# Row-sum reciprocals of an attention kernel sent through device memory instead of turned on TensorE, and the end of its perceptron done by row tile

## The chip, the cores and the metric

One Trainium2 chip, one core of it. The time is the device time of one execution in microseconds (us); a kernel is judged by the median of its runs. The engines are TensorE (PE: matrix products and turns, that is transposes, into PSUM), VectorE (DVE), ScalarE (ACT), GpSimd (POOL) and SyncE (SP), which issues all the transfers of this kernel, in program order, on one queue.

## What is computed

A decoder layer on x of 16 x 256 x 512 (self-attention, cross-attention on ctx_2048, each with 16 heads of 32 channels, then a perceptron of 512 to 2048 to 512), and behind it a "non-local" layer that multiplies by matrices made of ctx_2048. All in float32. Cut to what matters:

```
scores = einsum('bhqd,bhkd->bhqk', q, k) / sqrt(32)
scores = scores * mask - 10000.0 * (1.0 - mask)
probs  = softmax(scores)              # exp(s - max) / sum over the keys
ctx    = einsum('bhqk,bhkd->bhqd', probs, v)
x = x + merge_heads(ctx) @ w_o + b_o          # once for self-, once for cross-attention
x = x + gelu(layernorm(x) @ w1 + b1) @ w2 + b2
theta = theta_w @ x + theta_b ; out = gain * (w_w @ g^T phi^T theta / 512) + shift + x
```

The division by the sum is done last: the kernel weighs v with the raw exponentials, and multiplies the 32 channels of each head by 1/sum of their row. The sums stand with rows on the partitions, the weighed values with channels on the partitions, so the reciprocals must change sides.

## The kernel before

**Precision.** Every product of matrices is three products: each operand is split in a high part (`_h`) and the rest (`_l`), and `product` (L66 to L68) issues high*high, low*high and high*low.

**Blocks and slots.** The work is cut into 16 blocks k of two batches (512 rows): blocks 0 to 7 are self-attention, 8 to 15 cross-attention; k = 16 ends the last one. Each block has 8 slots h. In a slot every engine does, for several overlapping groups (a group is 4 heads of one batch, 128 groups in all), its next step: TensorE turns the exponentials of one group (L867, `turn`), does two units `a_` and `b_` of the projections (L66 to L68), scores a later group (L850), and weighs v with the turned exponentials (L880, `weigh`). Blocks 10 to 14 are one loop on the chip, the others are written out. The order within a slot is written by hand in the function `slot` of each engine, and waits are semaphores.

**PSUM.** Two banks, `banks`, go round: `a_`, `b_`, `own` (weigh), and so on. With three units in a slot, the bank that `weigh` filled in one slot is the one that `b_` needs in the next. `b_` therefore waits for `cx_ok`, which VectorE gives once it has read the weighed values out (`scaled`, L1384).

**Reciprocals.** In slot n VectorE takes the reciprocals of the 8 sums of each row (`inverses`, L1378, 128x8). GpSimd repeats each 32 times (`widen`, L657, tile `rwide`). At the end of `weigh` TensorE turns the two 128x128 halves of `rwide` into the free half of the bank (L884). In slot n+1 ScalarE copies them to `rt` (`sums_out`, L1112), and VectorE multiplies (`scaled`), ScalarE and VectorE split the result (`weighed`, L1118 and L1391).

**VectorE in a slot**: `mask_scores` part 0 (L1361), `inverses`, `scaled`, `maxima` part 0 (L1371), `weighed`, `mask_scores` part 1, the units' outputs, `maxima` part 1. TensorE's scores wait until both parts of `mask_scores` have emptied the PSUM tile `sc`.

**SyncE.** In slot 0 of a block it loads the rows of the block after it (`load_rows`, L441, four of 256 KB), in the cross-attention blocks also the context (`load_context`, L447, two of 512 KB) and the mask (`load_mask`, L452). `load_res` (L456) brings the rows that a result is added to, `store` (L460) writes the result.

**End.** After the attention come 8 bodies of the perceptron. After the last product of the last body VectorE adds four row tiles (L1587), ScalarE and VectorE split two batches of them and the two last `m1` matrices (`split_t`, L1246 to L1550), TensorE does `theta` and `last_product`, VectorE `last_out` (L1564), which for the last batch waits until the tile `res` has been stored.

Of the kernel before, what the change touches and what calls it, by code (L numbers as in the profile page):

```python
# [11 lines left out]
P = 128  # L12
# [125 lines left out]
def whole_network(nc, ctx, nl, m1t_dram, rows, x1, x2, ctx_t, s_mask, x_mask, s_weights, x_weights, fold_wt, columns, ln_biases,  # L138
# [19 lines left out]
    with ExitStack() as stack:  # L158
# [17 lines left out]
        b2_row = room.sb("b2_row", [P, 3 * H])  # L176
# [31 lines left out]
        with ExitStack() as shared:  # L208
            rt = shared.enter_context(nc.sbuf_tensor("A_rt", [P, S], F32))
        rwide = room.sb("rwide", [P, TPB, HPG, HD])  # L210
# [20 lines left out]
        w_s = rwide[:, :, :, :].rearrange("p t j d -> p t (j d)")  # L231
# [52 lines left out]
        def operands(b, end=False):  # L284

            whole = t_sb[:, b * TPB:(b + 1) * TPB, :]
            if end and b == BPB - 1:
                return (whole, x[:, 0, 0:S], (xt_h[:, 0:TPB, :], xt_l[:, 0:TPB, :]),
                        (xt_h[:, TPB, 0:S], xt_l[:, TPB, 0:S]), (xt_h[:, TPB + 1, :], xt_l[:, TPB + 1, :]))
            return whole, m1[:, :], (t_h[:, :, :], t_l[:, :, :]), (m1_h[:, :], m1_l[:, 0:S]), (thx_h[:, :], thx_l[:, :])  # L290

# [30 lines left out]
        inv_ok, wide_ok = room.sem("inv_ok"), room.sem("wide_ok")  # L322
        turned, pt_ok = room.sem("turned"), room.sem("pt_ok")
        rt_ok, cx_ok, c_hi, c_lo = (room.sem(n) for n in ("rt_ok", "cx_ok", "c_hi", "c_lo"))
# [6 lines left out]
        h_done, h_act, h_hi, h_lo = (room.sem(n) for n in ("h_done", "h_act", "h_hi", "h_lo"))  # L331
        a_done, t_bias, t_ok = room.sem("a_done"), room.sem("t_bias"), room.sem("t_ok")
# [94 lines left out]
        def _(sp):  # L427
# [54 lines left out]
            def store_out(blk, b, t):  # L482
                sp.wait_ge(y_ok, (blk + NU) * TT + (b * TPB + t + 1))
                sp.dma_start(row_tile(1, NU, NU + blk, b * TPB + t), y[:, t, :]).then_inc(st_y[t], DMA)
# [53 lines left out]
            def slot(r, k, h, a_, b_, own, pv):  # L538
                if k == 0 and h == 0:
# [12 lines left out]
                if h == 0:  # L552
# [14 lines left out]
                if h == 3 and NB <= k < NU:  # L567
                    load_mask(r, 1)
                if h == (5 if k < NU else 3) and k:
# [6 lines left out]
                if h == (7 if k < NU else 5):  # L576
                    if k:
                        for t in range(2):
                            store(k - 1, r - 1, t + 2)
                            if k < NU:  # L580
                                load_res(k, r, t)
# [7 lines left out]
                if k == NU and h == 5:  # L589
# [5 lines left out]
                    sp.dma_start(b2_row[:, 0:H], across(b2)).then_inc(ld_b2, DMA)  # L595
# [20 lines left out]
            def after(items):  # L616
                load_m1(NB - 1, 0)
                load_m1(NB - 1, 1)
                for b in range(BPB):
                    for t in range(TPB):  # L620
                        store_out(NB - 1, b, t)
# [5 lines left out]
        def _(pool):  # L627
# [23 lines left out]

            def widen(r, k, h):

                grp, _, g = group(r, h, -1)
                before_it = (c_lo, grp) if exists(k, h, -2) else ()
                wait_apart(pool, inv_ok, grp + 1, *before_it)
                pool.tensor_copy(rwide[:, :, :, :], rinv[:, g % 2, :, :].unsqueeze(3).to_broadcast([P, TPB, HPG, HD]))\  # L657
                    .then_inc(wide_ok, 1)
# [44 lines left out]
            def slot(r, k, h, a_, b_, own, pv):  # L703
# [3 lines left out]
                if own:  # L707
                    widen(r, k, h)
# [32 lines left out]
            def add_b2(blk):  # L741
                for t in range(TT):
                    pool.wait_ge(ld_t[t], (blk + 1) * DMA)
                    pool.tensor_tensor(t_sb[:, t, :], t_sb[:, t, :], b2_row[:, 0:H], ALU.add).then_inc(t_bias, 1)  # L744
# [11 lines left out]
        def _(pe):  # L756
# [114 lines left out]
            def weigh(r, h, bank):  # L871
# [5 lines left out]
                for c in range(TPB):  # L877
                    for j in range(HPG):
                        rr = slice(j * HD, (j + 1) * HD)
                        pe.matmul(banks[rr, bank, 0:S], v[:, b * TPB + c, f * P + j * HD:f * P + (j + 1) * HD],  # L880
                                  pt[:, j, c, :], start=(c == 0), stop=(c == TPB - 1))
                pe.wait_ge(wide_ok, grp + 1)
                for t in range(TPB):
# [763 lines left out]
```

## Time and profile before

| | |
|---|---|
| median of 3 runs | 2148.51 us (2147.06 to 2148.9) |
| the profiled execution, its own time | 2146.55 us |
| its span | 2144.6 us |
| TensorE busy | 2111.4 us, 98% |
| VectorE, ScalarE busy | 1396.8 us, 1203.9 us |
| granted TensorE clock, mean | 0.996 |
| moved by transfers | 126.24 MB, mean 59 GB/s |

The span is what the profile sees of the execution; 1.95 us lie around it. A busy share of 98% says that TensorE is what nearly everything waits for; where it isn't, the windows of the trace tell.

### The profile page before, as it was taken

What the parts mean: (1) busy time and instruction counts of PE and PEld (TensorE: products, weight loads), DVE (VectorE), ACT (ScalarE), POOL (GpSimd) and SP (SyncE); (2) the same over time, 40 slices, a digit from 0 to 9 for tenths busy, and PEclk for the clock granted to TensorE, in tenths of its full rate; (3) what the DMA queues carried; (4) which work ended last, traced back from release to release, by engine and by line L of the source; (5) the groups of instructions that cost most, each with busy time, mean ns of one, the idle gap of its engine ahead of it and who ended that gap; (6) DMA issues with size and microseconds to landing.
All of it is one profiled execution on the core that took longest, in us unless ns stands there. A gap on an engine that the chain in (4) does not pass through costs nothing.

```text
span 2144.6 us, 42719 instructions
## 1 busy us (share of the span) xinstructions
PE 2111.4 (98%) x14690; PEld 1684.0 (79%) x14690; DVE 1396.8 (65%) x3693; ACT 1203.9 (56%) x3396; POOL 465.7 (22%) x515
## 2 busy tenths in 40 slices
PE   8989999999999999999999999999999999999998
PEld 7867777777777777777777776778888888888886
DVE  7687877777778877787877879565343343435333
ACT  4387878777888888787887878521111111111111
POOL 1012021111114233223223221043031230313000
PEclk9999999999999999999999999999999999999999
DMA  8410110110121231122122021321101011101001
GB/s 281 137 46 21 40 60 21 41 60 27 35 99 55 75 105 55 51 74 70 38 68 83 24 79 65 106 85 45 42 22 44 20 44 39 40 24 44 22 23 44
DMA packets 77273, 126.24 MB, mean 59 GB/s; under 512 B 7504, under 2 KB 25040, under 8 KB 77136
## 3 DMA queue, kind: packets, MB, share of 16 engines
q1 hardware_dynamic: 77136, 124.45, 17.4%
q8 instruction: 81, 1.33, 0.3%
q14 instruction: 56, 0.46, 0.1%
HBM read 97.16 MB, written 27.26 MB: 58 GB/s over the span
## 4 chain that ended last, share of the span: by engine, by line
PE 91%; DVE 2%; issue 1%; DMA 0%; ACT 0%; DVEq 0%; ACTq 0%
PE A_banks L66 11%; PE A_banks L68 11%; PE A_banks L67 11%; PE A_tp L867 10%; PE A_banks L880 6%; PE A_sc L66 6%; PE A_sc L68 6%; PE A_sc L67 6%; PE A_tp L67 5%; PE A_tp L66 5%; PE A_tp L68 5%; PE A_sc L850 5%; PE A_banks L884 2%; PE A_tp L776 1%; DVE A_p L1371 1%
## 5 line engine op out<-in xcount | busy, mean ns | idle before, releaser
L1098 ACT ACTIVATE A_p<-A_p,A_nmax 128x256 f32<-128x256 f32 x1024 | 510.7, 510 | 0.0
L1361 DVE TENSOR_TENSOR A_p<-A_sc,A_mk 128x1024 f32<-128x1024 f32 x256 | 312.3, 1220 | 203.8 <-PE A_tp L867 203.8
L1104 ACT ACTIVATE A_pt<-A_tp 128x512 f32<-128x512 f32 x512 | 278.6, 596 | 235.9 <-PE A_tp L867 235.9
L1371 DVE CUSTOM_DVE_ANT_0 A_p<-A_p,A_ma 128x256 f32<-128x256 f32 x1024 | 381.1, 427 | 5.5
L867 PE MATMUL A_tp<-A_ident,A_p 128*128 128x128 f32 x2048 | 266.0, 273 | 1.4 <-ACT A_pt L1104 1.4
L867 PEld LDWEIGHTS A_tp<-A_ident,A_p 128*128 128x128 f32 x2048 | 235.0, 141 | 20.1 <-issue 2.4
L1098 ACT ACTIVATION_READ_ACCUMULATOR A_p<-A_p,A_nmax 128x1 f32 x1024 | 205.4, 201 | 0.0
L657 POOL COPY A_rwide<-A_rinv 128x256 f32<-128x256 f32 x128 | 51.4, 401 | 693.2 <-DVE A_ct_l L1391 693.2
L1231 ACT ACTIVATE A_mk<-A_tp,A_cols 128x512 f32<-128x512 f32 x62 | 42.7, 689 | 276.8 <-PE A_tp L68 276.8
L1231 ACT ACTIVATE A_ma<-A_tp,A_cols 128x512 f32<-128x512 f32 x62 | 42.7, 688 | 247.9 <-PE A_tp L68 247.9
L66 PE MATMUL A_banks<-A_xt_h,A_w_h 128*128 128x512 f32 x384 | 161.9, 421 | 0.0
L68 PE MATMUL A_banks<-A_xt_h,A_w_l 128*128 128x512 f32 x384 | 152.1, 396 | 0.0
L67 PE MATMUL A_banks<-A_xt_l,A_w_h 128*128 128x512 f32 x384 | 151.4, 394 | 0.0
L66 PE MATMUL A_tp<-A_xt_h,A_w_h 128*128 128x512 f32 x368 | 145.7, 396 | 0.0
L67 PE MATMUL A_tp<-A_xt_l,A_w_h 128*128 128x512 f32 x368 | 145.6, 396 | 0.0
L68 PE MATMUL A_tp<-A_xt_h,A_w_l 128*128 128x512 f32 x368 | 145.5, 395 | 0.0
L1533 DVE CAST A_h_h<-A_ma 128x512 fp32r<-128x512 f32 x64 | 31.5, 492 | 172.8 <-ACT A_ma L1231 169.0
L880 PE MATMUL A_banks<-A_pt,A_v 128*32 128x256 f32 x2048 | 139.0, 389 | 0.0
L1533 DVE CAST A_h_h<-A_mk 128x512 fp32r<-128x512 f32 x64 | 35.2, 549 | 158.9 <-ACT A_mk L1231 156.2
L744 POOL TENSOR_TENSOR A_v<-A_v,A_b_row 128x512 f32<-128x512 f32 x32 | 53.7, 1700 | 381.0 <-DMA A_v<-x 381.0
L66 PE MATMUL A_banks<-A_w_h,A_ct_h 128*128 128x512 f32 x256 | 107.5, 420 | 0.0
L67 PE MATMUL A_banks<-A_w_l,A_ct_h 128*128 128x512 f32 x256 | 100.9, 394 | 0.0
(223 smaller groups left out, 5032.3 us busy)
## 6 DMA issues: line engine op xcount, KB each, us to landing
A_x<-x SPq DMA_DIRECT2D x96, 256.0 KB, 3.7
A_res<-x SPq DMA_DIRECT2D x64, 256.0 KB, 2.7
x<-A_res SPq DMA_DIRECT2D x64, 256.0 KB, 2.3
A_e<-ctx SPq DMA_DIRECT2D x16, 512.0 KB, 4.2
A_e<-ctx_t SPq DMA_DIRECT2D x16, 512.0 KB, 6.5
A_e<-L_xattn_w SPq DMA_DIRECT2D x32, 256.0 KB, 3.1
A_v<-x SPq DMA_DIRECT2D x32, 256.0 KB, 2.8
out<-A_res SPq DMA_DIRECT2D x32, 256.0 KB, 2.0
```

What stands on the lines that cost most here:

```text
L66: pe.matmul(out, sh, mh, start=first, stop=False)
L67: pe.matmul(out, sh, ml, start=False, stop=False)
L68: return pe.matmul(out, sl, mh, start=False, stop=last)
L850: last = pe.matmul(sc[:, j, t * S:(t + 1) * S], qp[rr, f, rows_], kp[rr, f, keys], start=(n == 0), stop=(n == 2))
L867: last = pe.transpose(tp[:, j % 2, c * S + t * P:c * S + (t + 1) * P], p[:, g % 2, j, t, c * P:(c + 1) * P], ident[:, :])
L880: pe.matmul(banks[rr, bank, 0:S], v[:, b * TPB + c, f * P + j * HD:f * P + (j + 1) * HD], pt[:, j, c, :], start=(c == 0), stop=(c == TPB - 1))
L1098: act.activation(p[:, g % 2, j, t, :], p[:, g % 2, j, t, :], ACT.Exp, scale=-1.0, bias=nmax[:, g % 2, j, t:t + 1], accum_out=rsum[:, g % 2 ...
L1104: act.activation(pt[:, j, :, :], tp[:, j % 2, :].rearrange("p (c s) -> p c s", c=TPB), ACT.Copy)\
L1231: act.activation(hf[f % 4], hidden_bank(blk, f), ACT.Gelu_apprx_tanh, bias=b1_col[:, f:f + 1])\
L1361: dve.tensor_tensor(p[:, g % 2, heads, :, :].rearrange("p j t s -> p j (t s)"), sc[:, heads, :], m, ALU.mult)\
L1371: dve.tensor_tensor_reduce(out=a_, in0=a_, in1=ma[:, b, t, :], scale=-1.0, scalar=BIG, op0=ALU.add, op1=ALU.min, accum_out=nmax[:, g % 2, ...
L1533: dve.tensor_copy(h_h[:, f % 2, :], hf[f % 4]).then_inc(h_hi, 1)
```

## The change

The reciprocals change sides through device memory: SyncE stores the 128x8 tile `rinv` element by element (1024 elements of 4 bytes) as rows of a small tensor `inverses`, and loads from it, one transfer for each of four heads, each row repeated on 32 partitions, into `rt`. GpSimd's `widen`, TensorE's two turns and ScalarE's `sums_out` are gone. `scaled` now waits for the four loads (`ld_i`). `rt` becomes a tile of its own. In SyncE's slot the store comes first; `load_res`, which stood behind the stores of results, moves up behind it (to slots 0 and 6); the loads of the reciprocals come next, but in slots 0 and 3 behind the loads of rows, context and mask.

```diff
@@ SyncE
+            def store_inverses(r, h):
+                grp, _, g = group(r, h, -1)
+                wait_apart(sp, inv_ok, grp + 1, ld_i, (grp - 1) * HPG * DMA)
+                sp.dma_start(inv_dram[g % 2].rearrange("n s -> s n"), rinv[:, g % 2, :, :].rearrange("p t j -> p (t j)"),
+                             allow_slow_non_contiguous=True)\
+                    .then_inc(st_i, DMA)
+            def load_inverses(r, h):
+                grp, _, g = group(r, h, -1)
+                wait_apart(sp, st_i, (grp + 1) * DMA, cx_ok, grp)
+                for j in range(HPG):
+                    rr = slice(j * HD, (j + 1) * HD)
+                    own = inv_dram[g % 2].rearrange("(t j) s -> j t s", j=HPG)[j:j + 1]
+                    sp.dma_start(rt[rr, :].rearrange("p (t s) -> p t s", t=TPB), own.broadcast_to([HD, TPB, P]))\
+                        .then_inc(ld_i, DMA)
             def slot(r, k, h, a_, b_, own, pv):
+                if own:
+                    store_inverses(r, h)
+                if h == 0 and k > 1:
+                    for t in range(2):
+                        load_res(k - 1, r - 1, t)
+                if h == (6 if k < NU else 4) and k:
+                    for t in range(2):
+                        load_res(k - 1, r - 1, t + 2)
+                if own and h not in (0, 3):
+                    load_inverses(r, h)
...
                     if NB < k < NU:
                         load_mask(r, 0)
+                    if own:
+                        load_inverses(r, h)
...
                     for t in range(2):
                         store(k - 1, r - 1, t)
-                        load_res(k - 1, r - 1, t + 2)
...
@@ TensorE, weigh
-                pe.wait_ge(wide_ok, grp + 1)
-                for t in range(TPB):
-                    last = pe.transpose(banks[:, bank, S + t * P:S + (t + 1) * P],
-                                        rwide[:, t, :, :].rearrange("p j d -> p (j d)"), ident[:, :])
@@ VectorE
             def inverses(r, h):
+                wait(dve, st_i, (grp - 1) * DMA)
             def scaled(r, h, pv):
-                dve.wait_ge(rt_ok, grp + 1)
+                dve.wait_ge(done, pv[1])
+                dve.wait_ge(ld_i, (grp + 1) * HPG * DMA)
```

At the end, the last product's four row tiles each tell when they are done (`a_end`); VectorE adds and splits tile by tile, ScalarE too; the two `m1` matrices are split two steps earlier, beside the products; the first batch's last products go to the free PSUM tile `tp`, and the last batch's output to `x`, so that neither waits for a bank nor for a store:

```diff
@@ VectorE
             def after(items):
-                split_t(NB - 1, 0, True)
-                split_t(NB - 1, 1, True)
+                for t in range(TT):
+                    dve.wait_ge(a_end, t + 1)
+                    add_perceptron(NB - 1, t)
+                    if t == 2:
+                        split_end(0)
+                        split_end(1)
+                split_end(2)
+                split_end(3)
                 for item in items[:2]:
                     theta_out(item, NB, True)
```

What stands where, engine by engine. TensorE, at the end of a slot 7 and the start of the slot 0 after it (tiles by their names above, `A_` is the program's prefix), before:

```order
L880 MATMUL A_banks<-A_pt,A_v 32x256 [waits A_v_ok,A_pt_ok,A_y_ok]
L880 MATMUL A_banks<-A_pt,A_v 32x256 x7
L884 MATMUL A_banks<-A_ident,A_rwide 128x128 [waits A_wide_ok]
L884 MATMUL A_banks<-A_ident,A_rwide 128x128
L867 MATMUL A_tp<-A_ident,A_p 128x128 [waits A_x_lo,A_pt_ok,A_exped]
```

and of the change, there:

```order
L908 MATMUL A_banks<-A_pt,A_v 32x256 [waits A_v_ok,A_pt_ok,A_y_ok]
L908 MATMUL A_banks<-A_pt,A_v 32x256 x7
L895 MATMUL A_tp<-A_ident,A_p 128x128 [waits A_x_lo,A_pt_ok,A_exped]
L895 MATMUL A_tp<-A_ident,A_p 128x128 x3
L895 MATMUL A_tp<-A_ident,A_p 128x128 [waits A_x_lo,A_pt_ok,A_exped]
```

The two turns and their wait are gone; nothing takes their place on TensorE.

SyncE, from the end of block 8 to the first slots of block 9, before (block 9's slot 0 begins with the `A_x` loads; the second of the two masks belongs to slot 3):

```order
L460 DMA x<-A_res 128x512 [waits A_y_ok]
L456 DMA A_res<-x 128x512 [waits A_st_y1]
L441 DMA A_x<-x 128x512 [waits A_x_lo] x4
L447 DMA A_e<-ctx_t 128x4x256 [waits A_ctx_lo,A_et_lo] x2
L452 DMA A_mk<-mask_Bx1xSxS_ff 128x2x256 [waits A_biased] x2
```

and of the change (slot 0 begins with the first `inverses` store, slot 1 with the second):

```order
L470 DMA x<-A_res 128x512 [waits A_y_ok] x2
L499 DMA inverses<-A_rinv 128x8x1 [waits A_ld_i,A_inv_ok]
L466 DMA A_res<-x 128x512 [waits A_st_y0]
L466 DMA A_res<-x 128x512 [waits A_st_y1]
L451 DMA A_x<-x 128x512 [waits A_x_lo] x4
L457 DMA A_e<-ctx_t 128x4x256 [waits A_ctx_lo,A_et_lo] x2
L462 DMA A_mk<-mask_Bx1xSxS_ff 128x2x256 [waits A_biased]
L510 DMA A_rt<-inverses 32x2x128 [waits A_cx_ok,A_st_i]
L510 DMA A_rt<-inverses 32x2x128 x3
L499 DMA inverses<-A_rinv 128x8x1 [waits A_ld_i,A_inv_ok]
```

All the loads of slot 0 now stand behind a store that waits for this slot's reciprocals, both loads of `A_res` stand among them, and the four loads that `scaled` waits for stand last.

## Rows read from the trace of the kernel before

**Rows 1.** The page: span, TensorE's busy time, the chain that ended last by engine.

```profile
span 2144.6 us, 42719 instructions
...
PE 2111.4 (98%) x14690; PEld 1684.0 (79%) x14690; DVE 1396.8 (65%) x3693; ACT 1203.9 (56%) x3396; POOL 465.7 (22%) x515
...
PE 91%; DVE 2%; issue 1%; DMA 0%; ACT 0%; DVEq 0%; ACTq 0%
```

**Rows 2.** Windows: from:to us, length, busy time of each engine, clock, DMA share, GB/s.

```profile
200.00:300.00 100.00, 100.00 (x867) 78.46 (x867) 76.65 (x241) 79.25 (x242) 18.78 (x27) 1.00 0.14 44
1200.00:1400.00 200.00, 194.97 (x1503) 151.64 (x1501) 147.44 (x418) 145.10 (x428) 35.68 (x45) 0.98 0.24 82
```

**Rows 3.** Timeline of TensorE, block 11, slot 1: start, us, instruction.

```profile
938.64 1.07 PE L880 MATMUL A_banks<-A_pt,A_v 128*32 128x256 f32 x16
939.64 0.44 PE L884 MATMUL A_banks<-A_ident,A_rwide 128*128 128x128 f32 x2
939.91 1.04 PE L867 MATMUL A_tp<-A_ident,A_p 128*128 128x128 f32 x8
...
942.88 1.04 PE L867 MATMUL A_tp<-A_ident,A_p 128*128 128x128 f32 x8
943.67 0.48 PE L66 MATMUL A_banks<-A_xt_h,A_w_h 128*128 128x512 f32 x1
...
944.45 0.39 PE L66 MATMUL A_banks<-A_et_h,A_w_h 128*128 128x512 f32 x1
...
947.34 0.39 PE L850 MATMUL A_sc<-A_k_h,A_q_h 32*128 32x256 f32 x4
```

**Rows 4.** Timeline of SyncE's queue, block 11, slot 0.

```profile
932.28 0.33 SPq L456 DMA_DIRECT2D A_res<-x  x1
933.21 2.10 SPq L441 DMA_DIRECT2D A_x<-x  x4
935.65 1.09 SPq L447 DMA_DIRECT2D A_e<-ctx_t  x2
937.06 0.37 SPq L452 DMA_DIRECT2D A_mk<-mask_Bx1xSxS_ff  x1
```

**Rows 5.** DMA issues there: tile<-source, count, KB, median us from issue to landing.

```profile
A_mk<-mask_Bx1xSxS_ff SPq DMA_DIRECT2D x1, 256.0 KB, 6.7
```

**Rows 6.** Timeline of VectorE, block 11, slots 0 and 1.

```profile
932.52 0.19 DVE L1378 RECIPROCAL A_rinv<-A_rsum 128x8 f32<-128x8 f32 x1
...
942.24 0.37 DVE L1384 TENSOR_TENSOR A_cx<-A_banks,A_rt 128x256 f32<-128x256 f32 x1
...
944.75 1.21 DVE L1361 TENSOR_TENSOR A_p<-A_sc,A_mk 128x1024 f32<-128x1024 f32 x1
```

**Rows 7.** DMA of the whole execution: queue, packets, MB, share; issues and landings.

```profile
q1 hardware_dynamic: 77136, 124.45, 17.4%
...
x<-A_res SPq DMA_DIRECT2D x64, 256.0 KB, 2.3
...
A_m<-m1t SPq DMA_DIRECT2D x15, 128.0 KB, 2.7
...
A_m<-theta_t SPq DMA_DIRECT2D x1, 128.0 KB, 3.1
```

**Rows 8.** Windows around two stops of TensorE, columns as in rows 2.

```profile
1324.20:1326.10 1.90, 0.03 (x1) 0.00 (x0) 1.90 (x11) 1.90 (x7) 0.00 (x0) 1.00 0.19 71
...
1326.50:1329.80 3.30, 3.30 (x39) 2.52 (x41) 3.16 (x11) 3.30 (x13) 0.36 (x1) 0.50 0.63 210
...
2127.00:2130.70 3.70, 0.00 (x0) 0.01 (x1) 3.70 (x6) 2.40 (x4) 0.00 (x0) 1.00 0.00 0
...
2132.00:2135.40 3.40, 3.40 (x10) 2.56 (x9) 1.18 (x3) 0.96 (x2) 0.00 (x0) 0.50 0.00 0
```

**Rows 9.** Timeline of the end: last sums, ScalarE's split, TensorE's restart, last output.

```profile
2126.98 2.48 DVE L1587 TENSOR_TENSOR A_v<-A_sc,A_v 128x512 f32<-128x512 f32 x4 [3.59 <-PE A_sc L68]
2128.30 1.06 ACT L1246 ACTIVATE A_t_h<-A_v 128x1024 fp32r<-128x1024 f32 x1 [6.10 <-DVE A_v L1587]
...
2135.85 0.75 DVE L1556 SCALAR_TENSOR_TENSOR A_xt_l<-A_banks,A_cols,A_xt_h 128x512 fp32r<-128x512 f32 x1 [1.86 <-ACT A_xt_h L1253]
...
2140.58 0.75 DVE L1564 SCALAR_TENSOR_TENSOR A_res<-A_banks,A_fix,A_v 128x512 f32<-128x512 f32 x1 [0.43 <-DMA out<-A_res]
```

More of the change, by code:

```diff
@@ L568, in slot @@
                     load_mask(r, 1)
+                if own and h == 3:
+                    load_inverses(r, h)
                 if h == (5 if k < NU else 3) and k:
@@ L993, in hidden, with second @@
                 last.then_inc(h_done, 1)
-            def second(blk, f, first):
+            def second(blk, f, first, end=False):
                 if first:
@@ L1007, in second @@
                                    (hi, lo), f == 0, f == FT - 1)
-                last.then_inc(a_done, 1)
+                    if end:
+                        last.then_inc(a_end, 1)
+                if not end:
+                    last.then_inc(a_done, 1)
             def theta(item, blk, end=False):
@@ L1012, in theta @@
                 m_occupy((kind, b, rel), bank, blk)
-                pe.wait_ge(t_lo, (blk + rel) * BPB + (b + 1))
+                if not end:
+                    pe.wait_ge(t_lo, (blk + rel) * BPB + (b + 1))
                 pe.wait_ge(m1_lo, 1)
@@ L1025, in last_product @@
                 tb = blk + unit[2]
-                m_occupy(unit, bank, blk)
+                if not (end and b == 0):
+                    m_occupy(unit, bank, blk)
                 pe.wait_ge(m1_lo, tb * BPB + (b + 2))
@@ L1030, in last_product @@
                 cols_ = slice(o * P, (o + 1) * P)
-                product(pe, banks[:, bank, :], (mh[:, cols_], ml[:, cols_]), thx, True, True).then_inc(m_done, 1)
+                product(pe, unit_bank(item, end), (mh[:, cols_], ml[:, cols_]), thx, True, True).then_inc(m_done, 1)
             def m_slot(blk, f, first, last, unit, turns):
@@ L1045, in m_slot @@
                         m_turn(item, blk, False)
-                    second(blk, f, first)
+                    second(blk, f, first, last)
             def after(items):
@@ L1105, in turned_out @@
                     .then_inc(pt_ok, 1)
-            def sums_out(r, h, pv):
-                grp, _, g = group(r, h, -2)
-                bank, count = pv
-                act.wait_ge(done, count)
-                wait(act, cx_ok, grp)
-                act.activation(rt[:, :], banks[:, bank, S:2 * S], ACT.Copy).then_inc(rt_ok, 1)
             def weighed(r, k, h):
@@ L1265, in m_slot @@
                     m_turned(item, blk)
+                if last and f == FT - 2:
+                    split_fold(blk, 0, True)
+                    split_fold(blk, 1, True)
             def after(items):
-                split_t(NB - 1, 0, True)
-                split_t(NB - 1, 1, True)
+                for t in range(TT):
+                    split_end(t)
                 for item in items[:2]:
@@ L1562, in last_out @@
                 dve.wait_ge(m_done, count)
-                dve.wait_ge(st_y[o], (NU * 2 + tb * BPB + b) * DMA)
-                dve.scalar_tensor_tensor(y[:, o, :], banks[:, bank, :], fix[:, o:o + 1], t_sb[:, b * TPB + o, :],
+                if not (end and b == BPB - 1):
+                    dve.wait_ge(st_y[o], (NU * 2 + tb * BPB + b) * DMA)
+                dve.scalar_tensor_tensor(y_tile(b, o, end), unit_bank(item, end), fix[:, o:o + 1], t_sb[:, b * TPB + o, :],
                                          ALU.add, ALU.add).then_inc(y_ok, 1)
@@ L1581, in m_slot @@
                     m_turned(item, blk)
-                if f == FT - 1:
+                if last and f == FT - 2:
+                    split_fold(blk, 0, True)
+                    split_fold(blk, 1, True)
+                if f == FT - 1 and not last:
                     n = blk * FT + f
```

104 lines of the change are left out of this document (59 added, 45 removed).

## The prediction

> **What bounds the kernel now.** I read the page first: TensorE is busy 2111.4 us of a span of 2144.6, and the chain that ended last is 91% TensorE [rows 1]. An average over stages does not say where this holds, so the windows come next. From 200 to 300 us, in the attention, TensorE has no gap at all, while VectorE works 77 and ScalarE 79 us of 100; only the last 200 us of the attention have gaps, 5 us in all [rows 2]. So in the attention a microsecond less work on TensorE is a microsecond less time, as long as no other engine and no transfer comes later than TensorE does. Then I read one slot closely, slot 1 of block 11, because all slots repeat. It begins at 939.91 with the turns and the next would begin at 949.5 (9.6 us). Within it `b_` begins at 944.45 and the scores at 947.34 [rows 3]. These are the two places where TensorE could be held: `b_` needs the bank that `scaled` empties (942.24 + 0.37 = 942.61), the scores need `mask_scores` part 1 to have ended (944.75 + 1.21 = 945.96) [rows 6]. The covers are 1.84 and 1.38 us. `scaled` stands ahead of both on VectorE, so **it may come 1.4 us late for nothing, and beyond that every microsecond is TensorE's.** What `scaled` waits for is now the transfers; so SyncE's queue is the third thing to read.
>
> **Removed: the two turns.** The pair of L884 takes from 939.64 to 939.91, 0.27 us, until L867 can start; eight equal turns take 942.88 to 943.67, 0.79 us, so two of them 0.20 [rows 3]. The truth is between, since something of the switch from the narrow products to the turns stays: I take 0.22. 128 groups make 28 us (bounds 25 and 35). The five last groups lie in the stretch with gaps [rows 2] and give nothing: minus 1, 27 us. `sums_out` (ScalarE) and `widen` (GpSimd) are worth nothing, because neither engine is what TensorE waits for.
>
> **Added: the round trip, in an ordinary slot.** The reciprocals are ready 2.4 us into a slot (932.52 + 0.19 against a slot start of 930.30, which is 939.91 less 9.61) [rows 3, 6]. `scaled` takes them one slot later: 942.24, or 942.02 when the slot is 0.22 shorter. That is 9.3 us. The store: a store of 256 KB lands after 2.3 us [rows 7]; this one is 1024 packets, 64 for each of 16 engines. The trace has no such packets. From below they cost nothing, from above the mean packet of the execution: 0.174 x 2144.6 x 16 / 77136 = 77 ns [rows 7], so 64 take 5.0 us. They carry next to no data, so I take 1.3 us, near the lower end. Landing by about 3.5 us, then four issues at 0.35 to 0.4 us each [rows 4], then a landing like that of the 128 KB loads, 2.7 to 3.1 us [rows 7]: some 8.5 us. It fits into 9.3 plus 1.4. Ordinary slots cost nothing, also with the upper price only just.
>
> The Trainium skill ("DMA: Bandwidth & Descriptors", section Bandwidth, Measured) gives a floor of about 10.5 ns a packet. By an estimate from that page the store's 64 packets take 0.67 us, and the sum below would come out about 6 us lower. Its Specifications say that transfers under 512 B cost a read-modify-write, which speaks for more than the floor; no run so far shows either.
>
> **Added: the round trip in slot 0 of a block.** Here the order decides. Before, the transfers of slot 0 of block 11 are issued from 932.28 (`A_res`) to 937.06 (mask) [rows 4], and the mask lands 6.7 us after its issue [rows 5], at 943.76. A transfer of that size alone lands after 2.3 to 3.1 us [rows 7], so the mask waited behind what was issued before it: the queue is served in order, and is 11.5 us from first issue to last landing for 2.5 MB. In the change this queue (a) cannot begin before the reciprocals' store, at 932.75 and not 932.28; (b) has the store's 1.3 us ahead; (c) has a second `A_res` of 256 KB in it, 0.9 us (the 2.5 MB less the latency of some 2.3 us take 9.2 us); and (d) the four loads stand behind the mask. So the mask lands at 932.75 + 1.3 + 11.5 + 0.9 = 946.4. The loads are 256 packets of 512 B, as the `theta_t` load is, which landed 0.4 us later than loads of half as many packets [rows 7]; I take 0.9 (0.4 to 1.6, since they are four transfers). They land at 947.3, and `scaled` wanted them at 942.0. **5.3 us late, of which 1.4 are covered: TensorE stops for 3.9 us** at `b_` and a little at the scores of slot 1. Queued behind `scaled` on VectorE are `maxima` part 0, `weighed` and `mask_scores` part 1; ScalarE stands at `weighed`, with its turns 2 and 3 behind; SyncE itself is free again and the next slot's store is not late.
>
> Block by block: 9 to 14 have this whole queue, 6 x 3.9 = 23.4 us. 7 and 8 have no mask (0.9 less, and 2.9 or 3.0 left): 5.8. Block 1 has four rows, four turned weights and one shift row of 256 KB, nine units of 256 KB where block 11 will have eleven, so 2 x 0.9 less: about 2. Blocks 2 to 6 have six units: 4.5 us less, under a microsecond late, covered. Block 15 has seven (its other loads come behind the reciprocals): 1.7 late, 0.3 left. Sum 31.4 us.
>
> **The clock.** After TensorE stood 3.7 us from 2127.0, it ran from 2132.0 to 2135.4 at a granted 0.50, the 1.2 GHz level; after a stop of 1.9 us at 1324.2 again 3.3 us at 0.50 [rows 8]. Such a stretch costs half its length, 1.7 us. Stops of 3.9 us in six blocks: 10.2. Of the three shorter ones I count one half to two thirds: 1.8. Together 12 us (bounds 0 and 15).
>
> **The end.** Before, the four sums start at 2126.98 all together, the last output ends at 2140.58 + 0.75 = 2141.33 [rows 9]. By tile, with the products 0.68 us apart, the first sum can start at about 2124.95; ScalarE splits a tile in 0.53 (half of 1.06) and VectorE adds in 0.62 (a quarter of 2.48) [rows 9]. Following VectorE's order: three sums to 2126.9, two splits of 0.62 to 2128.2, a sum, two splits to 2130.0, `theta`'s low parts to 2130.8 and 2132.4 (each 0.75 after ScalarE's 0.70), then four outputs of 0.75 one after the other to 2135.4, none waiting for a bank or a store. That is 5.9 us earlier; I take 5.8. The two early splits of `m1` are 0.4 us each, in a stretch where VectorE is mostly idle.
>
> **Sum**, against the profiled execution's own 2146.55: -27 - 5.8 + 31.4 + 12 = 2157.2. The median of the three runs lies 1.96 above that execution, so 2159.
>
> **Rivals.**
> *The transfers hide after all* (chance 0.30 with all its degrees). If the loads land by 943.4 in block 11, 3.9 us earlier than I think, nothing stops: 2146.55 - 32.8 + 1.96 = 2116. For it: over the whole execution the queue is busy 17% only [rows 7], and a wait that vanishes in 119 of 128 slots might be cheap in nine. It turns to faster where the nine stops and their clock together fall below 32.8 - 4.3 = 28.5 us, with stops of about 2.3 us in place of 3.9. Against it: the mask alone landed at 943.76 before, with an earlier start and a shorter queue [rows 4, 5].
> *The store's small packets are dear* (0.10). At 77 ns a packet the store takes 5.0, 3.7 us more than I took: nine stops grow by 33, and blocks 2 to 6 and 15 stop for 2 to 4 us each with their clock, 22 more: 2214. From about 6.5 us to landing every slot would stop, 119 us for each microsecond.
> *TensorE isn't relieved* (0.10): the stops and the clock are small, but VectorE or the moved `load_res` (later by a slot's wait) take the place, and the time stays within a few microseconds of 2148.5. Against it: VectorE and ScalarE have over 20 us of 100 free [rows 2].
>
> **How the numbers follow.** This kernel can be told from no change at about 0.2%, 4.3 us. The forecast (0.50, stops eat the whole gain) has its own range: with a store of 0 and no clock loss 2135, with store 2.5 and all clocks 2175; 0.42 of it slower, 0.08 within. Hidden in part or whole: 0.29 faster, 0.01 within. Dear store: 0.10 slower. Third rival: 0.04 faster, 0.05 within, 0.01 slower. Together faster 0.33, within 0.14, slower 0.53. The range for 8 in 10 reaches from the wholly hidden case to short of the dear store: 2114 to 2195.
>
> **What the profile after would show.** Right: no L884; ordinary slots 9.39 us; in slot 1 of blocks 7 to 14 TensorE idle for 3 to 4 us at the first product of `b_`, released by VectorE's `A_cx`, and VectorE released by a DMA into `A_rt`; the granted clock at 0.50 after most of them; the mask of slot 0 landing 2 to 3 us later in the block than before; 5 to 6 us less between the last product of the perceptron and the end. Wrong, if `A_rt` lands before 1.4 us past `scaled`'s old place in these slots, if the small store takes over 5 us, or if ordinary slots are longer than 9.4 us.

## The result and the profile after

The changed kernel takes 2714.98 us (median of 4 runs, 2710.49 to 2730.67) against 2147.78 us before it on the same chip (4 runs, 2145.76 to 2148.9): 1.2655 times as long, 95% interval 1.2603 to 1.2707. The forecast was 2159 us, range 2114 to 2195. The sign was right, the size wrong by 556 us. Its profiled execution has a span of 2711.6 us. The page after it, the parts that answer to [rows 1] and [rows 7]:

```profile
span 2711.6 us, 42826 instructions
...
PE 2249.2 (83%) x14434; PEld 1739.0 (64%) x14434; DVE 1402.9 (52%) x3695; ACT 1177.6 (43%) x3270; POOL 417.6 (15%) x387
...
q1 hardware_dynamic: 251216, 141.79, 22.4%
...
PE 43%; DMA 34%; issue 7%; SPq 7%; ACT 2%; DVE 2%; another core or an unknown queue 1%; DVEq 0%; ACTq 0%
```

TensorE was 91% of the chain; now it is 43, and transfers are 34. It has 256 instructions fewer and is yet busy 138 us longer; the windows show a lower clock beside it, and where (columns as in [rows 2]; the first is all of the attention's slots, up to the end of the last `weigh`, the second the rest):

```profile
114.77:1930.72 1815.95, 1375.64 (x10332) 1022.40 (x10328) 999.79 (x3060) 980.68 (x2945) 238.07 (x229) 0.88 0.25 49
1930.72:2711.60 780.88, 769.57 (x3356) 622.20 (x3352) 321.97 (x481) 148.34 (x231) 168.66 (x139) 0.99 0.13 41
...
1930.72:1960.00 29.28, 23.43 (x88) 18.47 (x85) 8.58 (x15) 8.73 (x14) 2.52 (x2) 0.82 0.41 81
```

The same stretches before:

```profile
114.60:1366.57 1251.97, 1240.13 (x10589) 969.14 (x10585) 992.60 (x3060) 1007.31 (x3072) 286.81 (x359) 1.00 0.18 58
1366.57:2144.60 778.03, 767.45 (x3354) 620.67 (x3353) 323.06 (x479) 147.94 (x230) 168.30 (x137) 1.00 0.12 41
```

In the attention TensorE now stands still for 1816.0 - 1375.6 = 440 us, where it stood for 12. It is busy 136 us longer; without the turns (28 us) it should be 28 less, so the clock, 0.88 instead of 1.00, costs by an estimate some 164 us. (A little of it may not be the clock. A product is recorded at 0.39 us though the next begins after 0.23, so the last one before each stop adds 0.16 us of busy time, some 14 us over 90 stops.) 428 + 164 - 28 = 564 of the 567 us. The other 3 lie behind the attention: one more stop of 29.28 - 23.43 = 5.9 us with slow products behind it, less the gain of the new end.

What is it waiting for? The table of waits, SyncE's first row and TensorE's first (total us, times, longest):

```profile
SPq L35 <- DMA inverses<-A_rinv: 1089.2, 119, 11.7
...
PE A_banks L66 <- DVE A_cx L1422: 360.0, 90, 16.8
```

SyncE waits in nearly every slot for its own small store, 9.2 us in the mean. The chain of one such slot (block 11, slot 3; start, us, what):

```profile
1334.08 0.20 DVE A_rinv L1415
...
1334.33 8.91 DMA inverses<-A_rinv
...
1344.60 4.97 DMA A_rt<-inverses
...
1349.59 0.43 DVE A_cx L1422
...
1350.07 0.50 PE A_banks L66
```

The reciprocals are ready at 1334.28. Their 4 KB need 8.9 us until SyncE may issue the loads, which land at 1349.57 (the last takes 5.0 us here, where the median of these loads is 2.6). The slot in which `scaled` uses them began at 1341.21, and `scaled` would be due 2.4 us into it. TensorE:

```profile
1345.57 0.39 PE L68 MATMUL A_banks<-A_xt_h,A_w_l 128*128 128x512 f32 x1
1350.07 0.50 PE L66 MATMUL A_banks<-A_et_h,A_w_h 128*128 128x512 f32 x1 [4.11 <-DVE A_cx L1422]
...
1350.90 0.63 PE L66 MATMUL A_banks<-A_et_h,A_w_h 128*128 128x512 f32 x1
```

It stops for 4.1 us at the first product of `b_`, the place that the prediction named, and then runs products of 0.63 us in place of 0.40.

What does the store do in its 8.9 us? The view of transfers from 1334.30 to 1336.00 has all its packets, 1024 for the pieces and 16 more; in the window behind it the last column but one, the share in which the transfer engines are busy, is 0.00:

```profile
DMA packets 1040, 0.00 MB, mean 2 GB/s; under 512 B 1040, under 2 KB 1040, under 8 KB 1040
...
1336.00:1343.20 7.20, 7.20 (x68) 5.39 (x67) 4.95 (x13) 4.67 (x16) 0.00 (x0) 1.00 0.00 0
```

So by the profile the packets are over 1.7 us after the issue, and 7.2 us pass in which nothing moves until the store counts as landed. The time isn't in the packets but behind them.

A window over slot 2, which had all it needed, and slot 3:

```profile
1331.80:1341.20 9.40, 9.40 (x84) 7.27 (x80) 7.76 (x24) 7.77 (x23) 0.00 (x0) 1.00 0.08 6
1341.20:1356.50 15.30, 11.19 (x84) 8.37 (x80) 8.32 (x25) 7.65 (x23) 0.00 (x0) 0.89 0.20 26
```

Two things of the forecast are visible here: a slot without a stop is 9.40 us (9.61 before), and a stop costs more than itself, 1.8 us of slower products. A late slot gives the next group's transfers more time, so long and short slots often take turns.

### The profile page after: what moved, and what is told of

Read it like the earlier page. It is cut to its first block, busy times and chain, and to the rows that moved or that the text cites. A ratio compares the mean times of both kernels' runs of the same rounds, so it can differ in the third digit from the quotient of the medians.

```text
span 2711.6 us, 42826 instructions
## 1 busy us (share of the span) xinstructions
PE 2249.2 (83%) x14434; PEld 1739.0 (64%) x14434; DVE 1402.9 (52%) x3695; ACT 1177.6 (43%) x3270; POOL 417.6 (15%) x387
## 4 chain that ended last, share of the span: by engine, by line
PE 43%; DMA 34%; issue 7%; SPq 7%; ACT 2%; DVE 2%; another core or an unknown queue 1%; DVEq 0%; ACTq 0%
DMA inverses<-A_rinv 29%; DMA A_rt<-inverses 5%; PE A_sc L66 4%; PE A_sc L68 4%; PE A_sc L67 4%; PE A_tp L66 4%; PE A_tp L67 4%; PE A_tp L68 4%; PE A_banks L66 4%; SPq L510 4%; PE A_banks L68 4%; PE A_banks L67 4%; PE A_tp L895 3%; PE A_banks L908 1%; PE A_sc L878 1%
## 5 line engine op out<-in xcount | busy, mean ns | idle before, releaser
L1422 DVE TENSOR_TENSOR A_cx<-A_banks,A_rt 128x256 f32<-128x256 f32 x128 | 53.3, 417 | 516.4 <-issue 331.3
L895 PE MATMUL A_tp<-A_ident,A_p 128*128 128x128 f32 x2048 | 282.4, 281 | 34.4 <-ACT A_pt L1135 32.3
L1142 ACT ACTIVATE A_ct_h<-A_cx,A_bias_sum 128x256 fp32r<-128x256 f32 x128 | 65.5, 512 | 541.4 <-DVE A_cx L1422 540.0
L66 PE MATMUL A_banks<-A_xt_h,A_w_h 128*128 128x512 f32 x384 | 177.7, 463 | 98.4 <-DVE A_cx L1422 85.1
L66 PE MATMUL A_banks<-A_w_h,A_ct_h 128*128 128x512 f32 x256 | 124.7, 487 | 96.3 <-DVE A_cx L1422 89.4
L683 POOL TENSOR_TENSOR A_res<-A_res,A_o_bias 128x512 f32<-128x512 f32 x64 | 80.8, 1281 | 646.7 <-DVE A_nmax L1407 356.0
L66 PE MATMUL A_banks<-A_et_h,A_w_h 128*128 128x512 f32 x128 | 64.8, 506 | 129.9 <-DVE A_cx L1422 129.9
L67 PE MATMUL A_banks<-A_xt_l,A_w_h 128*128 128x512 f32 x384 | 162.6, 423 | 0.0
L68 PE MATMUL A_banks<-A_xt_h,A_w_l 128*128 128x512 f32 x384 | 162.1, 422 | 0.0
L66 PEld LDWEIGHTS A_banks<-A_xt_h,A_w_h 128*128 128x128 f32 x384 | 79.7, 208 | 124.4 <-DVE A_cx L1422 94.3
```

Of the source, the lines that this page charges most:

```text
L66: pe.matmul(out, sh, mh, start=first, stop=False)
L67: pe.matmul(out, sh, ml, start=False, stop=False)
L68: return pe.matmul(out, sl, mh, start=False, stop=last)
L683: pool.tensor_tensor(res[:, t % 2, :], res[:, t % 2, :], o_bias[:, int(k >= NB), :], ALU.add)\
L895: last = pe.transpose(tp[:, j % 2, c * S + t * P:c * S + (t + 1) * P], p[:, g % 2, j, t, c * P:(c + 1) * P], ident[:, :])
```

## The experiments

Two questions: why does a store of 4 KB take over 9 us, and was the rest of the forecast sound? "Wait" below is SyncE's mean wait for the store by the table of waits; "landing" is the median from issue to landing between 400 and 600 us, where the view of DMA issues gives one. Both are read in the profiled execution.

**1. The same bytes in 128 pieces.** The eight values of a partition lie side by side in device memory:

```diff
-sp.dma_start(inv_dram[g % 2].rearrange("n s -> s n"), rinv[...] ...)
+sp.dma_start(inv_dram[g % 2].rearrange("n s -> (n s)").rearrange("(s n) -> s n", n=TPB * HPG), rinv[...] ...)
```

> The changed kernel, with the store of the reciprocals written as 128 pieces of 32 bytes (the eight of one partition side by side) in place of 1024 of 4 bytes; bytes, issues, waits and loads are the same, but the reciprocals reach wrong rows, so the output isn't the reference's. Theory A (the cost is that of each small write to device memory): the store of after, which let its loads be issued 10.4 us after its own issue, shrinks to about 3 us; ordinary slots are 9.39 us, and the time is what the forecast said for slot 0 of nine blocks, 2130 to 2175 us. Theory B (a fixed wait between a store to device memory and what waits for it): still about 10 us, and 2650 to 2720 us. Slot-0 queue as forecast: TensorE stops 3 to 4 us in slot 1 of blocks 9 to 14 and the granted clock falls to 0.50 after it (2157 us); if the loads land in time there, about 2116 us.

Measured: 2151.81 us against 2147.84, ratio 1.0022 (1.0011 to 1.0032). The store lands after 1.4 us. The reciprocals reach wrong rows here, so this kernel serves for its time alone. It isn't a fixed wait (theory B): the way in which 4 KB are written carries all but 4 us of the loss. And this kernel is the one that the forecast had in mind, with a store of 1.3 us. Its slot 1 of block 11 began at 940.48. SyncE, VectorE and TensorE there:

```profile
934.10 0.33 SPq L499 DMA_DIRECT2D inverses<-A_rinv  x1
...
939.78 0.37 SPq L462 DMA_DIRECT2D A_mk<-mask_Bx1xSxS_ff  x1
940.35 2.31 SPq L510 DMA_DIRECT2D A_rt<-inverses  x4
...
947.39 0.42 DVE L1422 TENSOR_TENSOR A_cx<-A_banks,A_rt 128x256 f32<-128x256 f32 x1 [4.44 <-DMA A_rt<-inverses]
...
947.87 0.50 PE L66 MATMUL A_banks<-A_et_h,A_w_h 128*128 128x512 f32 x1 [2.62 <-DVE A_cx L1422]
```

The landing of the mask there (last column, us):

```profile
A_mk<-mask_Bx1xSxS_ff SPq DMA_DIRECT2D x1, 256.0 KB, 6.9
```

And windows over slot 1 of block 9 and of block 11:

```profile
777.84:791.58 13.74, 11.22 (x84) 8.17 (x81) 9.01 (x25) 8.16 (x24) 2.43 (x3) 0.88 0.39 123
...
940.48:952.78 12.30, 9.68 (x84) 7.21 (x80) 6.96 (x24) 6.99 (x23) 0.62 (x1) 1.00 0.46 146
```

The mask lands at 946.7, 15.6 us into slot 0 (931.10), where it was 13.5 before and 16.1 in the forecast. `scaled` comes 4.5 us late (forecast 5.3) and TensorE stops 2.6 us at `b_` (forecast 3.9). In slot 1 of blocks 9, 10 and 12 to 14 the clock is 0.88 after such a stop, in block 11 it is not, although its stop is as long.

**2. Half the pieces.** Only the first row tile's four columns are stored, and used for both.

```diff
-inv_dram[g % 2].rearrange("n s -> s n"), rinv[:, g % 2, :, :].rearrange("p t j -> p (t j)")
+inv_dram[g % 2, 0:HPG].rearrange("n s -> s n"), rinv[:, g % 2, 0, :]
```

> The changed kernel, with only the first row tile's four columns stored (512 pieces of 4 bytes) and loaded for both row tiles, so the second tile is scaled by the first's reciprocals. Theory A (each piece costs the same): the 8.5 us behind the last packet halve, store to loads about 6 us, close under the 6.5 us that a slot can bear: 2160 to 2260 us. Theory B (fixed): 10 us and about 2700 us. Theory C (pieces that share a block of device memory hold each other up): as A here, since each row's pieces still lie side by side.

Measured: 2623.56 us, ratio 1.2215. The waits:

```profile
SPq L35 <- DMA inverses<-A_rinv: 821.5, 105, 11.4
```

7.8 us a wait in place of 9.2: half the pieces save a sixth. Theory A, in which each costs the same, is wrong. So is what theory C was said to give here, the same 2160 to 2260 us: each row's pieces lie as close as before, and the wait has hardly changed.

**3. The pieces apart.** All 1024 pieces again, each 512 bytes from the next. The loads keep their shape but bring a weight's values instead, here and in experiments 7 and 10.

```diff
-nc.dram_tensor("inverses", [2, TPB * HPG, P], F32, kind="Internal")
+nc.dram_tensor("inverses", [2, TPB * HPG, P, P], F32, kind="Internal")    # written at [..., 0]
```

> The changed kernel, with each of the 1024 pieces of 4 bytes written 512 bytes from the next one, into a tensor 128 times as large; the loads have their old shape, but read from a weight, so the values are wrong. Theory A (each small write costs, wherever it goes): store to loads 10 us or more, 2700 us or more. Theory C (neighbours in one block of memory are written one after the other): 3 to 5 us, and under 2250 us.

Measured: 2162.96 us, ratio 1.0070 (1.0050 to 1.0090). The same number of the same small writes lands in 2.6 us:

```profile
inverses<-A_rinv SPq DMA_DIRECT2D x21, 4.0 KB, 2.6
```

One of these stores, issued at 177.98, has the same packets in the same time as the one above, here from 177.90 to 179.60, and has landed 2.7 us after its issue:

```profile
DMA packets 1040, 0.00 MB, mean 2 GB/s; under 512 B 1040, under 2 KB 1040, under 8 KB 1040
```

So it is neighbours in device memory that cost, and they cost behind the packets. This run decides against theory A.

**4. A tile on the chip as the place of exchange.**

```diff
+for t in range(TPB):
+    for j in range(HPG):
+        sp.dma_start(inv_row[row:row + 1, t * P:(t + 1) * P], rinv[:, g % 2, t, j:j + 1], ...)
...
-own = inv_dram[g % 2] ...
+own = bass.AP(line.tensor, line.offset, [[S, 1], [0, HD], [1, S]])      # one line of inv_row, 32 times
```

> The changed kernel, with the reciprocals written to a tile on the chip (eight stores, one for each row of 128 elements of 4 bytes, 1024 pieces in all) and loaded from there by four loads that repeat a row 32 times; the same values, nothing left out. Theory A in its form 'it is device memory that is slow for small writes': eight issues of 0.38 us and about 2 us to land, 5 us; ordinary slots just fit, nine slot-0 stops are longer than forecast: 2150 to 2230 us. If it is the transfer engines that are slow for each small piece, whatever they write to: 11 to 13 us and 2750 us or more.

Measured: 2477.43 us, ratio 1.1544 (1.1513 to 1.1574), between the two forecasts, 2150 to 2230 and over 2750 us; neither came true. The issues of one round and the landings over the whole execution:

```profile
899.87 5.03 SPq L503 DMA_DIRECT2D A_inv_row<-A_rinv  x8
...
A_inv_row<-A_rinv SPq DMA_DIRECT2D x1024, 0.5 KB, 2.3
A_rt<-A_inv_row SPq DMA_DIRECT2D x512, 32.0 KB, 4.5
```

A row of 128 touching pieces lands on the chip after 2.3 us, so there neighbours do no harm. The round is long for two other reasons: the eight issues take SyncE 5 us, and four loads that read a single partition 32 times land after 4.5 us where those from device memory take 1.9 (experiment 1).

**5. The end of the perceptron alone**, in the kernel before: the second part of the diff and nothing of the first.

> The kernel before, with the second part of the change alone: the end of the perceptron by row tile. The forecast priced it at -5.8 us, whatever the transfers do: 2142 us against 2147.8. If the shorter end is given back (the outputs' stores land last, or the two early splits of m1 stand in the way of the last body), 0 to -3 us.

Measured: 2140.99 us (6 runs, 2140.7 to 2142.12) against 2147.48, ratio 0.9970 (0.9958 to 0.9982): -6.5 us. VectorE's first sums and its last outputs there, answering to [rows 9]:

```profile
2125.18 2.05 DVE L1597 TENSOR_TENSOR A_v<-A_sc,A_v 128x512 f32<-128x512 f32 x3 [1.55 <-PE A_sc L68]
...
2134.17 1.40 DVE L1612 SCALAR_TENSOR_TENSOR A_x<-A_banks,A_fix,A_v 128x512 f32<-128x512 f32 x2
```

The first sum starts at 2125.18 (forecast 2124.95) and the last output ends at 2135.57 (2135.4).

**6. The loads of the reciprocals first**, in experiment 1's kernel: ahead of rows, context and mask in slots 0 and 3.

```diff
-if own and h not in (0, 3):
+if own:
     load_inverses(r, h)
...
-    if own:
-        load_inverses(r, h)          # and the same behind load_mask(r, 1) in slot 3
```

> The run with 128 pieces of 32 bytes (whose reciprocals reach wrong rows), with the four loads of the reciprocals put ahead of the rows, the context and the mask in slots 0 and 3 of a block. Theory of the queue: the slots 1 of blocks 1 and 7 to 14, which are 2 to 5 us longer than 9.4 us each in that run and some 35 us in all, go back to 9.4, and the time is 2113 to 2122 us. Rival (the loads are late there because the first transfers of slot 0, the rows that a result is added to, and the traffic itself slow them): the slots stay 2 us or more too long and the time is 2130 us or more.

Measured: 2121.18 us, ratio 0.9883 (0.9868 to 0.9898). It is 30.6 us below experiment 1. The windows over slots 0 and 1 of block 11:

```profile
919.30:928.68 9.38, 9.38 (x84) 7.28 (x80) 7.07 (x23) 7.64 (x23) 1.17 (x1) 1.00 0.50 150
928.68:938.10 9.42, 9.42 (x85) 7.30 (x81) 8.05 (x25) 7.74 (x23) 0.88 (x2) 1.00 0.63 202
```

No gap is left in slot 1, with the same traffic: the order in the queue made the stops. The same holds in blocks 7 to 14. Only block 1 stays long there (12.8 us, 10.5 in experiment 1), where the turned weights are loaded too. TensorE's busy time over the whole falls from 2094.6 us in experiment 1 to 2081.9 with the same instructions, so some 12.7 of the 30.6 us were the clock.

**7. 32 bytes apart** (the tensor's last size is 8).

> The changed kernel, with each of the 1024 pieces of 4 bytes written 32 bytes from the next one (the loads read a weight instead, the values are wrong). Pieces 512 bytes apart gave 2163 us. Theory C with blocks of at most 32 bytes: store to loads 2.4 to 2.8 us and 2163 us again. Theory C with blocks of 64 bytes or more: still 5 us or more, over 2300 us.

Measured: 2172.93 us, ratio 1.0116 (1.0098 to 1.0135); wait 2.5 us, landing 2.7. Nearly what 512 bytes gave (2.4 and 2.6), so pieces 32 bytes apart all but leave each other alone. The time is 10 us above that of experiment 3 and the two intervals don't meet, so a small cost may be left.

**8. A layout that keeps all values**: 256 pieces of 16 bytes, loads first.

```diff
-rinv = room.sb("rinv", [P, 2, TPB, HPG])
+rinv = room.sb("rinv", [P, 2, HPG, TPB])                # PIECE = 4 values: two heads, two row tiles
...
+sp.dma_start(inv_dram[g % 2]....rearrange("(m s n) -> s m n", s=P, n=PIECE), ...)
...
+at, size = divmod(j * TPB, PIECE)[0] * P * PIECE + j * TPB % PIECE, P * PIECE - PIECE + TPB
+sp.dma_start(rt[rr, 0:size], own.broadcast_to([HD, size]))          # own = the flat tensor from `at`
...
+rt[:, 0:P * PIECE].rearrange("p (s n) -> p n s", n=PIECE)[:, 0:TPB]     # what `scaled` reads
```

> Nothing left out: the loads stand first as in the run before, the reciprocals are laid out by head and then by row tile, so that the store is 256 pieces of 16 bytes (the values of two heads in two row tiles), and each load brings 2 KB, from where its head's values start, of which VectorE reads every fourth or so. If two pieces in each 32 bytes hold each other up only once, store to loads is 2 to 3 us, all slots are 9.39 us, and the time is 2115 to 2125 us, faster than both kernels. If it is the number of pieces that share 512 bytes (here 32, in the changed kernel 128) that counts, about 4 us, which fits too; only over 6.5 us would the time rise above 2150.

Measured: 2132.33 us, ratio 0.9923 (0.9908 to 0.9938); landing 2.3 us. It is faster than both kernels, though by 15 us and not the 22 to 32 expected: `scaled` takes 0.56 us with the strided operand, and slots 2 and 3 of some blocks are still up to 1.5 us too long (block 9's slot 3 takes 10.9).

**9. 512 pieces of 8 bytes**, four in each 32, `PIECE = 2`.

> Nothing left out: as the run with 256 pieces of 16 bytes, but with 512 pieces of 8 bytes (one head's value in two row tiles), four in each 32 bytes, and loads of 1 KB, no more than needed. SyncE's mean wait for the store was so far 9.2 us with 8 pieces in each 32 bytes, 7.8 us with 8 in each but half as many pieces, 2.0 us with 2, 1.4 us with 1, and 2.3 to 2.5 us for 1024 pieces with 32 bytes or more each. Theory D: what costs is how many pieces follow each other into the same 32 bytes, about 1.0 to 1.1 us each: 4.0 to 5.0 us here. Theory N: the pieces count, not their neighbours: near 7.8, as in the run with as many pieces. By D ordinary slots fit narrowly, and the time is 2120 to 2140 us; by N over 2500 us.

Measured: 2159.86 us, ratio 1.0054 (1.0037 to 1.0071). The wait is 442.4 / 127 = 3.5 us, landing 3.8. The expectation's 4 to 5 was somewhat too much; 7.8, for as many pieces with eight in each 32 bytes, is far off. The time is outside the 2120 to 2140 us expected with it, though: there are still stops, here in slot 2, since the store of slot 1 is behind the traffic of slot 0.

**10. 4 bytes in every 8** (last size 2).

> The changed kernel, with each of the 1024 pieces of 4 bytes written 8 bytes from the next one, so four in each 32 bytes (the loads read a weight instead, the values are wrong). Theory D: SyncE's mean wait for the store is 2.4 us and three times 1.0 to 1.1, 5.4 to 5.7 us, and the time 2180 to 2300 us. If only pieces that touch each other are slow, about 2.4 us, and 2165 to 2175 us.

Measured: 2216.07 us, ratio 1.0324 (1.0303 to 1.0345):

```profile
inverses<-A_rinv SPq DMA_DIRECT2D x20, 4.0 KB, 4.4
```

The pieces don't touch and still cost, though less than theory D said: the wait is 430.5 / 111 = 3.9 us, where 5.4 to 5.7 were expected. That only touching pieces are slow (2.4 us) is wrong too.

**11. The context's loads later**, in experiment 8's kernel: from slot 0 to slot 2.

```diff
-    if NB <= k + 1 < NU:                        # in slot 0
-        load_context(r + 1)
+if h == 2 and NB <= k + 1 < NU:                 # behind load_inverses
+    load_context(r + 1)
```

> Nothing left out: the run with 256 pieces of 16 bytes, with the two loads of the context (1 MB) moved from slot 0 to slot 2 of a block, behind the reciprocals' loads; GpSimd needs them in slots 5 and 7. In that run slots 2 and 3 of blocks 9 to 11 were still 0.1 to 1.5 us too long, because the small transfers of slot 1 came behind slot 0's 2.5 MB. If that is why, they go back to 9.4 and the time falls by 3 to 5 us to about 2128; if it only moves the stop to slot 3, no change.

Measured: 2124.06 us (2122.08 to 2127.34) against 2145.92, ratio 0.9900 (0.9884 to 0.9917). The wait is 213.9 / 120 = 1.8 us, the landing 2.1. It is the fastest version that leaves nothing out: 22 us below the kernel before. Slots 2 and 3 of blocks 9 to 14 are 9.4 us again.

**12. One store for each row**, to device memory.

> The changed kernel, with the store to device memory cut into eight, one for each row of 128 elements of 4 bytes, as the run that wrote to a tile on the chip had it; the same values, nothing left out. There each of the eight landed 2.3 us after its issue, and the eight issues took 5 us. Here each transfer again puts eight pieces into each 32 bytes of device memory, but is alone in its row. Theory D (pieces that go into the same 32 bytes of device memory wait for each other, about 1 us each): each lands after 8 us or more, and the time is 2700 us or more. Rival (it was the pieces of eight different rows, written in turn, that held each other up): each lands after 2 to 3 us as on the chip, and the time is 2300 to 2450 us, since the issues alone still take 5 us of SyncE.

Measured: 2986.6 us, ratio 1.3903 (1.3791 to 1.4014). SyncE's issues of one round, and its waits, here behind the last of the eight issues:

```profile
1085.49 3.68 SPq L502 DMA_DIRECT2D inverses<-A_rinv  x8
...
1096.96 3.67 SPq L512 DMA_DIRECT2D A_rt<-inverses  x4
...
SPq L35 <- DMA inverses<-A_rinv: 927.5, 119, 10.9
```

Another 7.8 us behind the last issue, though each transfer is one row, where the rival wanted 2 to 3. The stores are those of experiment 4, where each landed after 2.3 us and SyncE waited 157.5 / 107 = 1.5 us behind the last; only their target differs. So it doesn't help to take the rows one by one. How long one row alone would take is not shown: the eight are issued within 3.7 us and are under way together, and whether rows under way together disturb each other stays open.

Together:

| pieces | size, distance | in each 32 bytes | wait, us | landing, us | time, us |
|---|---|---|---|---|---|
| 128 | 32, touching | 1 | 1.4 | 1.4 | 2151.8 |
| 1024 | 4, 512 apart | 1 | 2.4 | 2.6 | 2163.0 |
| 1024 | 4, 32 apart | 1 | 2.5 | 2.7 | 2172.9 |
| 256 | 16, touching | 2 | 2.0 (1.8 in 11) | 2.3 (2.1) | (8, 11) |
| 512 | 8, touching | 4 | 3.5 | 3.8 | (9) |
| 1024 | 4, 8 apart | 4 | 3.9 | 4.4 | 2216.1 |
| 512 | 4, touching | 8 | 7.8 | not given | 2623.6 |
| 1024 | 4, touching | 8 | 9.2 | not given | 2715.0 |

(Experiments 8, 9 and 11 have another order of loads, so their times aren't compared here.) The waits not shown above, from the same view: experiments 1, 3, 7, 8, 9 and 10, in this order (us in total, times, longest).

```profile
SPq L35 <- DMA inverses<-A_rinv: 127.5, 94, 6.3
SPq L35 <- DMA inverses<-A_rinv: 256.2, 109, 6.8
SPq L35 <- DMA inverses<-A_rinv: 273.0, 109, 6.9
SPq L35 <- DMA inverses<-A_rinv: 235.9, 118, 6.7
SPq L35 <- DMA inverses<-A_rinv: 442.4, 127, 7.4
SPq L35 <- DMA inverses<-A_rinv: 430.5, 111, 8.0
```

Down the third column the wait grows from 1.4 to 2.5 us up to 9.2; at the same value of that column, twice to eight times the pieces add 0.4 to 1.4.

## Why the prediction was wrong

**The step that failed: the price of the store.** The forecast took 1.3 us, "near the lower end", because the pieces "carry next to no data", with 5.0 us as the upper bound (64 mean packets of 77 ns), and landing by about 3.5 us. It is 9 us and more, outside both bounds. As a price of the packets 1.3 us was not far off (they are over within 1.7 us of the issue); what the sum had no term for is the 7 us between the last packet and the landing. The bound was a mean over the kernel's packets, most of them large; "dear" was thought of as a price for each packet. The runs show that the number of pieces matters little (experiments 2, 3) and the number that share a small stretch of device memory matters most (3, 7, 9, 10). Why such neighbours land late is open.

The Trainium skill ("DMA: Bandwidth & Descriptors", section Bandwidth, Measured) gives its 10.5 ns a packet as time in which the transfer engines are busy, measured on loads issued by GpSimd. The trace agrees in kind, with this store's 1040 packets over 1.7 us after its issue. But the figure doesn't tell when another transfer may rely on a store. The read-modify-write under 512 B of its Specifications speaks for a cost, but as a threshold it doesn't fit: pieces 32 bytes apart (2.7 us) land like those 512 bytes apart (2.6). Whether it is what pieces within the same 32 bytes wait for, no run shows.

The upper bound was also misread. The forecast wrote that ordinary slots cost nothing "also with the upper price only just". In its own terms a landing by 3.5 us with a store of 1.3 is one by 7.2 us with a store of 5.0, above the 6.5 from which every slot stops: (7.2 - 6.5) x 119 = 83 us, which the "dear store" with its 2214 us left out.

**"Ordinary slots cost nothing"** fell with it. The rival "dear store" said that from about 6.5 us to landing every slot would stop, 119 us for each microsecond. By the mean wait, 9.2 us plus the issue's 0.4, that is (9.6 - 6.5) x 119 = 369 us; TensorE stood 428 us more. The mechanism was right, for a chance of 0.10 and a time that assumed 5.0. Experiment 10 (4.4 us) and experiment 2 (7.8 us plus the issue) lie on either side of that bend: 2216 and 2624 us. The line itself doesn't hold there. For experiment 2 it gives (8.2 - 6.5) x 119 = 202 us, but TensorE stands 384 us in its attention:

```profile
114.60:1838.10 1723.50, 1339.53 (x10332) 1003.76 (x10329) 998.39 (x3060) 977.39 (x2945) 234.70 (x229) 0.89 0.23 52
```

So the nearness of 369 and 428 is in part luck. The loads land later in that run (median 3.0 us against 2.6 in the changed kernel and 1.9 in experiment 1), which the 6.5 didn't allow for; whether that is all isn't shown.

**The clock** was priced for nine stops (12 us). With 90 stops at `b_` alone it is some 164 us, over a third on top of the 428 in which TensorE stands.

**Slot 0 of a block: right in mechanism, a little large.** With a store as cheap as assumed (experiment 1), slots 1 of blocks 9 to 14 are 3 to 5 us longer than 9.4, block 8's 3.7, block 7's 2.1, block 1's 1.1 (slots are measured from their first turn to the next slot's), those of blocks 2 to 6 not at all; experiment 6 removes all of it in blocks 7 to 14 by order alone. Stops and clock were forecast at 31.4 + 12 = 43.4 us; experiments 1 and 6 differ by 30.6, of it clock some 12.7. The stop itself was mis-sized: `scaled` was 4.5 us late in block 11, not 5.3, and what covers it is the 1.84 us up to `b_`, not the 1.4 up to the scores, because VectorE catches up before the scores. 4.5 - 1.84 = 2.7 against 2.62 measured.

**The turns: right.** 0.22 us a slot was forecast, and slots without a stop went from 9.61 to 9.39 or 9.40. With that the rival "TensorE isn't relieved" falls; "the transfers hide after all" came true only in another order (experiment 6). One reading under this term was too narrow: the attention's gaps, 11.8 us in all, are not only in its last 200 us (5.0). The other 6.8 lie between 114.6 and 192 us, so the first groups give less too, for eight of them at most 8 x 0.22 = 1.8 us.

**The end: right.** -5.8 forecast, -6.5 measured (experiment 5).

**The sum with the store set right**: for experiment 1's kernel the forecast's own 2159 stands against 2151.8. It is that near partly by luck. The stops were 13 us too dear, and small losses that it doesn't have make up for some of that: with no stop left in slots 1 of blocks 7 to 14, experiment 6 is 26.3 us faster than the kernel before, not the 27 + 6.5 of turns and end.

## What to carry to other kernels

- Before you send a column of a tile through device memory, count how many of its pieces fall into the same 32 bytes there. Here eight made 4 KB land after 9 us and more, one after 1.4 to 2.7. The packets don't tell: in the two stores looked at, touching and 512 bytes apart, they were over within 1.7 us. Write each partition's values side by side, and let the loads start at an offset and the reader take a stride.
- Price a round trip up to the wait that ends it, and ask how much slack each repetition has: past the slack every repetition pays, and TensorE's clock adds to it (here some 164 us on 428).
- In a queue served in order, a small transfer that is due goes ahead of large ones that are not (experiment 6, 31 us; experiment 11, 5 by the ratios or 8 by the medians).

## What was not expected of the hardware

- Writes of 4 bytes to device memory next to each other: 9.2 us mean wait for 1024; the same pieces 32 bytes apart 2.5 us; on the chip a row of 128 of them 2.3 us. Touching or 512 bytes apart, the 1040 packets were over within 1.7 us of the issue; the rest of the wait lies behind them. Whether it is the transfer engine or the memory that orders writes to one place was not tried, nor how the pieces of one 32 bytes are spread over the engines. 32 bytes is the smallest distance tried that is nearly free, 8 the largest tried that isn't; the true one may lie between. Growth isn't even: from 1 to 4 pieces about 1.4 us, from 4 to 8 another 5.
- Of stops of 2.5 to 2.6 us, some were followed by a clock of 0.88 over the slot and one (block 11 in experiment 1) by full speed. Of two stops of 1.8 us in the same run, block 8's was followed by 0.87 over the slot, block 7's by full speed. Why is open.
- Four loads that repeat one partition's line on 32 partitions landed after 4.5 us from the chip's own memory and after 1.9 us from device memory.
